# One maximum pass a head instead of one a pair of heads, in a fused attention and feed-forward block

## The chip, the cores and the metric

The kernel runs on one core of a Trainium2 chip. The metric is the device time of one execution in microseconds (us); several executions are timed and their median counts. One further execution is recorded by the hardware profiler. The engines are named as the profile names them: PE is TensorE (PEld its weight loads), DVE is VectorE, ACT is ScalarE, POOL is GpSimd, SP is the queue that issues the DMAs.

## The reference, cut to what matters

For each of 32 batches, `x` has 256 tokens of 128 features. The block normalises `x`, scales and shifts it, and computes an attention in which, for each of 16 heads, the keys and values are read as 8 x 256 matrices, so that the scores of one head are 256 x 256:

```python
q = (x @ Wq + bq).reshape(b, h, dh, t)          # h = 16, dh = 8, t = 256; k and v alike
attn = jnp.einsum('bhdt,bhds->bhts', k, v) * temperature
attn = jax.nn.softmax(attn, axis=-1)
out = jnp.einsum('bhdt,bhts->bhds', q, attn)
```

The result is gated and added to `x`. A second normalisation and a gated feed-forward layer follow, whose activations and weights are rounded block by block to a 4-bit grid, with a second gated residual. The change touches only the row maxima of the scores, which the softmax subtracts.

## The kernel before, in words

The program is a software pipeline over the batches, written out by hand. On each engine a function `step(k, m)` lists in a fixed order the tasks of step k; `at(k, m, lag, task)` runs the task for batch k - lag. So one step works on up to ten batches at once, each at another stage, and each engine executes its list strictly in order. Steps 0 to 11 and those from 32 on are written out; steps 12 to 31 are a hardware loop whose body holds four steps, so the loop turns back at steps 16, 20, 24 and 28. All ordering between engines is by semaphores: a task waits for counts and raises one at its end.

The scores of a head are 256 x 256. PE writes them in `scores` (L900) as two matmuls of 128 x 256 into one of the four slots of `score_ps[:, h % 4]`, a PSUM tensor of four banks, and raises `scored` once a head. A slot may be written again when the exponentials of the head four before are done (`exped`). DVE takes the negated row maxima in `maxes` (L650): pass u reads heads 2u and 2u+1 in one TENSOR_REDUCE of 1024 elements a partition, writes four columns of `neg_max` and raises `maxed`. ACT computes the exponentials in `exps` (L504), two activations of 256 elements a head, each with its row sum, and waits for `maxed` at even heads. PE multiplies them with the scaled queries in `mix` (L942).

The order on DVE in a step is: `var2` (L721), `hid_magic`, maxes 7 of the previous batch, `stats1_rows`, `v_hi`, maxes 0, `h2_max` (L616), `k_lo`, `gate2`, `stats1_end`, `v_lo`, `h2_scale`, maxes 1, `row_sums_inv` (L698), `silu` 0, `h2_recip` (L736), maxes 2, `h2_exponent` (L623), `var1`, `h2_magic`, `silu` 1, maxes 3, `times_up` twice (L757), maxes 4, `hid_max`, maxes 5, `hid_scale`, `gate1` (L704), `hid_recip` (L773), maxes 6, `stats2_rows`, `k_hi`, `stats2_end`, `hid_exponent`.

POOL takes part in a round trip with DVE once a step: `rstd2_pow` (L338) waits for the `ve` of `var2`; `normalise2`, `scale2` and `shift2` (L343, L349, L356) follow; `h2_max` on DVE waits for `shift2`. POOL goes on with `hid_add` and `hid_sub` (L414, L418), `q_scaled` (L369, waits for `row_sums_inv`) and `h2_y` (L389, waits for `h2_recip`); `h2_exponent` on DVE waits for `h2_y`.

On PE the pairs of scores stand between the projections, the transposes and the eight `mix` groups; on ACT the exponentials stand between seven evacuations and activations of other stages. The exponentials of heads 12 to 15 come at the head of the next step. SP issues the DMAs that pass the keys and values through DRAM (`split_dram`) into `k_stack` and `v_stack`, on which the first scores of a batch wait.

Of the kernel before, what the change touches and what calls it, by code (L numbers as in the profile page):

```python
# [10 lines left out]
AX = mybir.AxisListType  # L11

NB, T, D = 32, 256, 128
H, DH = 16, 8
# [19 lines left out]
def adaln_block(nc, x, wq, bq, wk, bk, wv, bv, temperature, w_gate, w_up, w_down, c, wmod, out):  # L34
    with ExitStack() as ctx:
        def sb(name, shape, dt=F32):
            return ctx.enter_context(nc.sbuf_tensor(name, shape, dt))

        def sem(name):
            return ctx.enter_context(nc.semaphore(name))  # L40
# [45 lines left out]
        neg_max = sb("neg_max", [128, 2, H * 2])  # L86
# [19 lines left out]
        score_ps = ctx.enter_context(nc.psum_tensor("score_ps", [128, 4, 2, T], F32))  # L106
# [27 lines left out]
        scored, maxed, exped = sem("scored"), sem("maxed"), sem("exped")  # L134
# [27 lines left out]
        def wait_batches(eng, s, n, per=1):  # L162

            if isinstance(n, int):
                n = min(n, NB)
                if n <= 0:
                    return
            eng.wait_ge(s, n * per)
# [300 lines left out]
        def _(act):  # L469
# [25 lines left out]

            def exps(b, c, h):
                p = c % 2
                if h % 2 == 0:
                    act.wait_ge(maxed, b * (H // 2) + h // 2 + 1)
                if h == 0:  # L500
                    wait_batches(act, mixed, b - 1)
                for a in range(2):
                    n = 2 * h + a
                    nc.scalar.activation(probs[p][:, h, a, :], score_ps[:, h % 4, a, :], ACT.Exp,  # L504
                                         bias=neg_max[:, p, n:n + 1],
                                         accum_out=row_sum[:, p, h, a:a + 1]).then_inc(exped, 1)
# [35 lines left out]
            def step(k, m):  # L542
                at(k, m, 3, exps, 12)
                at(k, m, 3, exps, 13)
                if isinstance(k, int) and k == 5:
                    ff_weights()
                at(k, m, 5, h2T_out)
                at(k, m, 7, hidT_out, 1)
                at(k, m, 3, exps, 14)
                at(k, m, 3, exps, 15)  # L550
                at(k, m, 1, q_out)
                at(k, m, 5, tanh, 0)
                at(k, m, 2, exps, 0)
                at(k, m, 2, exps, 1)
                at(k, m, 2, exps, 2)
                at(k, m, 2, exps, 3)
                at(k, m, 5, tanh, 1)
                at(k, m, 2, exps, 4)
                at(k, m, 2, exps, 5)
                at(k, m, 2, exps, 6)  # L560
                at(k, m, 2, exps, 7)
                at(k, m, 2, exps, 8)
                at(k, m, 2, exps, 9)
                at(k, m, 0, h_out)
                at(k, m, 6, hidT_out, 0)
                at(k, m, 2, exps, 10)
                at(k, m, 2, exps, 11)
# [5 lines left out]
        def _(dve):  # L573
# [69 lines left out]

            def maxes(b, c, u):
                p = c % 2
                dve.wait_ge(scored, b * H + 2 * u + 2)
                if u == 0:
                    wait_batches(dve, exped, b - 1, 2 * H)
                lo = 2 * (u % 2)
                nc.vector.tensor_reduce(neg_max[:, p, 4 * u:4 * u + 4],  # L650
                                        score_ps[:, lo:lo + 2, :, :].rearrange("p b a n -> p (b a) n"),
                                        AX.X, ALU.max, negate=True).then_inc(maxed, 1)

            def stats1_rows(b, c):
                wait_dma(dve, x_loaded, b, c)
# [137 lines left out]
            def step(k, m):  # L793
                if isinstance(k, int) and k == 0:
                    condition()
                at(k, m, 4, var2)
                at(k, m, 6, hid_magic)
                at(k, m, 3, maxes, 7)
                at(k, m, 0, stats1_rows)
                at(k, m, 1, v_hi)  # L800
                at(k, m, 2, maxes, 0)
                at(k, m, 4, h2_max)
                at(k, m, 1, k_lo)
                at(k, m, 7, gate2)
                at(k, m, 0, stats1_end)
                at(k, m, 1, v_lo)
                at(k, m, 4, h2_scale)
                at(k, m, 2, maxes, 1)
                at(k, m, 3, row_sums_inv)
                at(k, m, 5, silu, 0)  # L810
# [252 lines left out]
```

## Time and profile before

| what | us |
|---|---|
| median of 3 runs | 703.82 |
| lowest and highest of them | 703.37, 707.37 |
| the profiled execution | 700.42 |
| its span, first to last instruction | 698.6 |

The profiled execution is 1.8 us longer than its span and 3.4 us shorter than the median. Sums from the trace are made against 700.42 and then carried over to the median.

### The profile page before, as it was taken

To read this page: it belongs to the slowest core of one execution; us is meant where nothing else is said; L and a number is where in the kernel's file an instruction comes from. 1 tells how busy PE (TensorE), PEld (TensorE's weight loads), DVE (VectorE), ACT (ScalarE), POOL (GpSimd) and SP (SyncE) were. 2 spreads that over 40 slices of the span, in tenths; PEclk is the share of its full clock that TensorE was granted. 3 is DMA by queue.
4 is the path that set the end of the run, shared out by engine and by line. 5 is a ranking of instruction groups with operands and counts; after the bars stand their busy time and mean duration, and the time that the engine had idled before them with its cause. 6 is when DMAs were issued, how large, how long until landed. Compare 5 with 4: busy or idle time off the path is not lost.

```text
span 698.6 us, 17168 instructions
## 1 busy us (share of the span) xinstructions
PE 565.0 (81%) x4336; PEld 387.3 (55%) x4336; DVE 600.1 (86%) x1331; ACT 569.5 (82%) x2281; POOL 512.2 (73%) x655
## 2 busy tenths in 40 slices
PE   4577788888888988898888888798888888978673
PEld 2355354656566655665565656565556565645343
DVE  5578489999999999999998999999998999999452
ACT  2287599999998999889997999899997989999211
POOL 2114747888888788878887788878886887877884
PEclk9557799999999999989999999999998999999957
DMA  3544435555555555544554455644555455550000
GB/s 109 148 118 125 122 94 134 144 125 148 139 138 141 146 152 151 133 132 108 149 147 118 126 144 150 153 129 120 132 139 142 116 140 135 144 137 23 31 8 23
DMA packets 87855, 85.82 MB, mean 123 GB/s; under 512 B 8551, under 2 KB 83533, under 8 KB 87789
## 3 DMA queue, kind: packets, MB, share of 16 engines
q1 hardware_dynamic: 87344, 84.94, 46.6%
q14 instruction: 49, 0.39, 0.2%
q8 instruction: 18, 0.29, 0.2%
q10 hardware_dynamic: 444, 0.20, 0.1%
HBM read 47.29 MB, written 37.81 MB: 122 GB/s over the span
## 4 chain that ended last, share of the span: by engine, by line
POOL 26%; issue 24%; DVE 20%; PE 14%; ACT 6%; DMA 5%; SPq 3%; DVEq 1%; ACTq 1%; POOLq 1%
DVE neg_max L650 6%; ACT probs L504 5%; POOL hid_q L414 5%; PE score_ps L900 4%; POOL hid_q L418 4%; PE bank L942 4%; DVE hid L757 3%; POOL rstd L338 3%; DMA k_stack<-split_dram 3%; POOL q_z L369 2%; POOL h_c L349 2%; POOL h L356 2%; DVE hid_am L616 2%; POOL h_c L343 2%; POOL h_q L389 2%
## 5 line engine op out<-in xcount | busy, mean ns | idle before, releaser
L504 ACT ACTIVATE probs<-score_ps,neg_max 128x256 f32<-128x256 f32 x1024 | 471.7, 488 | 43.0 <-DVE neg_max L650 31.8
L650 DVE TENSOR_REDUCE neg_max<-score_ps 128x4 f32<-128x1024 f32 x256 | 310.3, 1213 | 21.6 <-PE score_ps L900 21.1
L900 PE MATMUL score_ps<-v_stack,k_stack 128*128 128x256 f32 x1024 | 220.8, 334 | 61.7 <-DMA k_stack<-split_dram 35.1
L900 PEld LDWEIGHTS score_ps<-v_stack,k_stack 128*128 128x128 f32 x1024 | 155.6, 201 | 134.7 <-ACT probs L504 96.8
L504 ACT ACTIVATION_READ_ACCUMULATOR probs<-score_ps,neg_max 128x1 f32 x1024 | 226.0, 221 | 0.0
L942 PE MATMUL bank<-probs,q_z 128*32 128x256 f32 x2048 | 140.8, 395 | 10.4 <-POOL q_z L369 10.3
L942 PEld LDWEIGHTS bank<-probs,q_z 128*32 128x32 f32 x2048 | 54.6, 111 | 64.8 <-POOL q_z L369 27.8
L962 PE MATMUL bank<-wgu_T,h_T 128*128 128x352 f32 x128 | 56.6, 529 | 24.7 <-DVE ffn_g L788 13.4
L991 PE MATMUL bank<-wd_T,hid_T 118*128 118x128 f32 x384 | 60.6, 299 | 4.8 <-ACT hid_T L538 4.3
L327 POOL TENSOR_TENSOR rstd<-ve,minus_half 128x2 f32<-128x2 f32 x32 | 22.7, 710 | 48.6 <-DVE ve L666 48.5
L991 PEld LDWEIGHTS bank<-wd_T,hid_T 118*128 118x128 f32 x384 | 52.5, 207 | 10.1 <-ACT hid_T L538 8.9
L338 POOL TENSOR_TENSOR rstd<-ve,minus_half 128x2 f32<-128x2 f32 x32 | 29.5, 921 | 37.5 <-DVE ve L721 37.5
L418 POOL TENSOR_TENSOR hid_q<-hid_q,hid_mag 128x704 f32<-128x704 f32 x32 | 53.9, 1683 | 2.5
L414 POOL TENSOR_TENSOR hid_q<-hid_q,hid_mag 128x704 f32<-128x704 f32 x32 | 53.7, 1677 | 2.4 <-DVE hid_mag L627 2.4
L538 ACT ACTIVATE hid_T<-bank 118x384 f32<-118x384 f32 x64 | 32.9, 516 | 23.2 <-PE bank L982 23.1
L971 PE MATMUL bank<-wgu_T,h_T 128*128 128x352 f32 x128 | 50.6, 483 | 0.8 <-DVE kv_lo L691 0.8
L369 POOL TENSOR_TENSOR q_z<-q_T,inv_sum 128x128 f32<-128x128 f32 x64 | 25.0, 411 | 32.6 <-DVE inv_sum L698 32.6
L396 POOL TENSOR_TENSOR hid_q<-hid,hid_rs 128x704 f32<-128x704 f32 x32 | 44.4, 1387 | 3.3 <-DVE hid_rs L773 2.6
L532 ACT ACTIVATE tanh_g<-bank 128x352 f32<-128x352 f32 x64 | 30.4, 475 | 17.4 <-PE bank L962 16.5
L423 POOL TENSOR_TENSOR hid_q<-hid_q,hid_sc 128x704 f32<-128x704 f32 x32 | 44.4, 1389 | 0.2
L377 POOL TENSOR_TENSOR x<-gated,x_in 128x256 f32<-128x256 f32 x32 | 23.2, 726 | 27.9 <-DVE gated L704 27.9
L920 PE MATMUL bank<-w_kv,hT 128*128 128x256 f32 x128 | 40.3, 409 | 1.3 <-ACT hT L514 1.3
(104 smaller groups left out, 919.8 us busy)
## 6 DMA issues: line engine op xcount, KB each, us to landing
split_dram<-kv_hi SPq DMA_DIRECT2D x128, 128.0 KB, 2.4
split_dram<-kv_lo SPq DMA_DIRECT2D x128, 128.0 KB, 2.7
v_stack<-split_dram SPq DMA_DIRECT2D x32, 512.0 KB, 4.3
k_stack<-split_dram SPq DMA_DIRECT2D x128, 128.0 KB, 4.6
mod_bc<-mod_dram SPq DMA_DIRECT2D x32, 256.0 KB, 3.7
x_in<-in_L_attn_x_dram SPq DMA_DIRECT2D x32, 128.0 KB, 3.4
out_dram<-out_t SPq DMA_DIRECT2D x32, 128.0 KB, 1.9
w_mod<-in_L_wmod_dram SPq DMA_DIRECT2D x1, 384.0 KB, 3.4
```

The source lines that it names most:

```text
L338: nc.gpsimd.tensor_tensor(rstd2[:, :], ve2[:, :], minus_half[:, :], ALU.pow).then_inc(rstd2_made, 1)
L396: nc.gpsimd.tensor_tensor(blocks16(hid_q[:, :], 2 * FF), blocks16(hid[:, :], 2 * FF), spread16(hid_rs[:, :], 2 * FF), ALU.mult).then_inc(h ...
L414: nc.gpsimd.tensor_tensor(hid_q[:, :], hid_q[:, :], hid_mag[:, :], ALU.add).then_inc(hid_t_made, 1)
L418: nc.gpsimd.tensor_tensor(hid_q[:, :], hid_q[:, :], hid_mag[:, :], ALU.subtract)\
L423: nc.gpsimd.tensor_tensor(blocks16(hid_q[:, :], 2 * FF), blocks16(hid_q[:, :], 2 * FF), spread16(hid_sc[:, :], 2 * FF), ALU.mult).then_inc ...
L504: nc.scalar.activation(probs[p][:, h, a, :], score_ps[:, h % 4, a, :], ACT.Exp, bias=neg_max[:, p, n:n + 1], accum_out=row_sum[:, p, h, a: ...
L650: nc.vector.tensor_reduce(neg_max[:, p, 4 * u:4 * u + 4], score_ps[:, lo:lo + 2, :, :].rearrange("p b a n -> p (b a) n"), AX.X, ALU.max, n ...
L900: last = nc.tensor.matmul(score_ps[:, h % 4, a, :], k_stack[p][:, h, 128 * a:128 * a + 128], v_stack[p][:, h // R, :], start=True, stop=True)
L942: last = nc.tensor.matmul(bank_mix[32 * g:32 * g + 32, 0:T], q_z[p][:, a, g, r, :], probs[p][:, R * g + r, a, :], start=(i == 0), stop=(i ...
L962: nc.tensor.matmul(bank_gate[a][:, 0:FF], h2_T[:, 128 * a:128 * a + 128], wgu_T[:, 0, :], start=True, stop=True).then_inc(gate_ps_made[a], 1)
L971: nc.tensor.matmul(bank_up[a][:, 0:FF], h2_T[:, 128 * a:128 * a + 128], wgu_T[:, 1, :], start=True, stop=True).then_inc(up_ps_made[a], 1)
L991: last = nc.tensor.matmul(bank_down[:, a * D:(a + 1) * D], hid_T[:, a, t, :], wd_T[:, t, :], start=(t == 0), stop=(t == HT - 1))
```

## The change

Each pass that took the maxima of two heads becomes two passes of one head: 512 elements a partition, two columns of `neg_max`, with a wait and a raised semaphore of their own. A batch has 16 passes in place of 8. ACT waits for `maxed` at every head in place of every second. The place of the passes in the DVE order stays: both halves of a pair stand where the pair stood. PE, POOL and SP are not changed.

```diff
             def exps(b, c, h):
                 p = c % 2
-                if h % 2 == 0:
-                    act.wait_ge(maxed, b * (H // 2) + h // 2 + 1)
+                act.wait_ge(maxed, b * H + h + 1)
...
             def maxes(b, c, u):
                 p = c % 2
-                dve.wait_ge(scored, b * H + 2 * u + 2)
-                if u == 0:
-                    wait_batches(dve, exped, b - 1, 2 * H)
-                lo = 2 * (u % 2)
-                nc.vector.tensor_reduce(neg_max[:, p, 4 * u:4 * u + 4],
-                                        score_ps[:, lo:lo + 2, :, :].rearrange("p b a n -> p (b a) n"),
-                                        AX.X, ALU.max, negate=True).then_inc(maxed, 1)
+                for h in (2 * u, 2 * u + 1):
+                    dve.wait_ge(scored, b * H + h + 1)
+                    if h == 0:
+                        wait_batches(dve, exped, b - 1, 2 * H)
+                    nc.vector.tensor_reduce(neg_max[:, p, 2 * h:2 * h + 2], score_ps[:, h % 4, :, :],
+                                            AX.X, ALU.max, negate=True).then_inc(maxed, 1)
```

## Rows read from the trace of the kernel before

**Rows 1.** the page's part 1: busy us, share of the span, instructions

```profile
PE 565.0 (81%) x4336; PEld 387.3 (55%) x4336; DVE 600.1 (86%) x1331; ACT 569.5 (82%) x2281; POOL 512.2 (73%) x655
```

**Rows 2.** DVE and ACT groups by shape: busy us, mean ns | idle before, releasers

```profile
L504 ACT ACTIVATE probs<-score_ps,neg_max 128x256 f32<-128x256 f32 x1024 | 471.7, 488 | 43.0 <-DVE neg_max L650 31.8 <-issue 8.3
L650 DVE TENSOR_REDUCE neg_max<-score_ps 128x4 f32<-128x1024 f32 x256 | 310.3, 1213 | 21.6 <-PE score_ps L900 21.1
...
L757 DVE TENSOR_TENSOR hid<-silu_g,bank 128x352 f32<-128x352 f32 x64 | 30.3, 513 | 0.5 <-PE bank L971 0.5
...
L616 DVE TENSOR_REDUCE h_am<-h 128x16 f32<-128x256 f32 x32 | 13.4, 418 | 16.4 <-POOL h L356 16.1
```

**Rows 3.** timeline of VectorE, one regular batch: start us, us, instruction [idle before]

```profile
321.73 0.42 DVE L616 TENSOR_REDUCE h_am<-h 128x16 f32<-128x256 f32 x1 [0.60 <-POOL h L356]
...
325.26 1.16 DVE L650 TENSOR_REDUCE neg_max<-score_ps 128x4 f32<-128x1024 f32 x1
326.45 0.29 DVE L623 TENSOR_SCALAR h_mag<-h_q 128x256 int32<-128x256 int32 x1
...
328.73 0.94 DVE L757 TENSOR_TENSOR hid<-silu_g,bank 128x352 f32<-128x352 f32 x2
329.59 1.22 DVE L650 TENSOR_REDUCE neg_max<-score_ps 128x4 f32<-128x1024 f32 x1
330.72 0.88 DVE L616 TENSOR_REDUCE hid_am<-hid 128x44 f32<-128x704 f32 x1
...
333.07 0.42 DVE L773 RECIPROCAL hid_rs<-hid_sc 128x44 f32<-128x44 f32 x1
333.47 1.22 DVE L650 TENSOR_REDUCE neg_max<-score_ps 128x4 f32<-128x1024 f32 x1
```

**Rows 4.** timeline of GpSimd and TensorE in the same batch

```profile
325.80 0.62 POOL L389 TENSOR_TENSOR h_q<-h,h_rs 128x256 f32<-128x256 f32 x1
...
332.71 0.72 PE L900 MATMUL score_ps<-v_stack,k_stack 128*128 128x256 f32 x4
```

**Rows 5.** the chain that ended last, a regular batch: start us, us, what

```profile
413.44 0.18 DVE ve L721
...
419.37 1.45 POOL hid_q L418
...
421.79 0.59 POOL h_q L389
...
432.19 0.18 DVE ve L721
```

**Rows 6.** timeline of VectorE, the instruction that writes ve at L721

```profile
108.92 0.17 DVE L721 TENSOR_SCALAR ve<-mv 128x2 f32<-128x2 f32 x1
...
373.76 0.17 DVE L721 TENSOR_SCALAR ve<-mv 128x2 f32<-128x2 f32 x1 [0.34 <-issue]
...
394.84 0.17 DVE L721 TENSOR_SCALAR ve<-mv 128x2 f32<-128x2 f32 x1
...
643.70 0.17 DVE L721 TENSOR_SCALAR ve<-mv 128x2 f32<-128x2 f32 x1
```

**Rows 7.** the chain at a turn of the loop

```profile
366.94 1.14 DVE neg_max L650
...
372.85 2.17 issue
...
377.11 0.80 PE score_ps L900 x2
...
391.21 0.18 DVE hid_sc L620
```

**Rows 8.** the chain while the pipeline fills

```profile
80.45 1.15 DVE neg_max L650
```

**Rows 9.** timeline of VectorE in the first step after the loop

```profile
577.68 1.23 DVE L650 TENSOR_REDUCE neg_max<-score_ps 128x4 f32<-128x1024 f32 x1 [0.27 <-PE score_ps L900]
```

**Rows 10.** timeline of VectorE in the turn step

```profile
380.69 0.73 DVE L620 TENSOR_SCALAR h_sc<-h_am 128x16 f32<-128x16 f32 x1
```

## The prediction, made before the changed kernel was timed

> **What bounds the kernel now.** I first read the engines' busy times [rows 1]: DVE leads with 600.1 us of 698.6, ACT and POOL have 569.5 and 512.2. A share alone doesn't say who sets the pace, so the second view is the length of one step, from one `ve` at L721 to the next. Between the rows at 108.92 and 643.70 [rows 6], the first and the last of 29 such rows, there are 28 steps. The 22 regular ones take 18.3 to 19.0 us, 410.5 us together. The four at which the loop turns take 21.1 to 21.6 (373.76 to 394.84 is one of them), and the steps that enter and leave the loop 19.7 each.
>
> Third comes the chain of waits through a regular step [rows 5]. It leaves DVE at `ve` (413.44), runs through POOL (second normalisation, `hid_sub` until 420.8, `h_q` at 421.79), comes back to DVE and stays there, with no stall of note, until the next `ve` at 432.19. So a regular step is one trip: some 8.9 us from `ve` to the end of `h_q`, all POOL's, then 9.8 us of DVE work. While POOL has the trip, DVE does its other work and has a little over: it sits idle 0.60 us before `h_am` [rows 3], and all such waits are 16.1 us [rows 2]. The second slack is negative: the pass of maxes 2 starts at 325.26 and `h_mag` at 326.45, 1.19 later, where the pass of maxes 4 lets its successor start after 1.13 (329.59 to 330.72) [rows 3]. The 0.06 is `h_mag` waiting for `h_q`, whose end is at 326.42 [rows 4]. ACT has 17.8 us of work in a step of 18.7 and isn't on the chain there.
>
> At a turn it is otherwise [rows 7]: the pass of maxes 4 (366.94) releases ACT, ACT works through until it stands still for 2.17 us of issue (372.85), then come its next exponentials, the scores of the new batch on PE (377.11) and PE's mixes, and DVE enters only at `hid_sc` (391.21).
>
> **The change: the price of a split pass on DVE.** A TENSOR_REDUCE takes 1213 ns for 1024 elements and 418 ns for 256 [rows 2], so 1.035 ns an element and about 0.15 us fixed; one of 512 should take 0.68 us. What a step pays is the distance between starts, not the duration. The pass at 329.59 lasts 1.22, and the next instruction starts after 1.13, 0.09 before its end. The two passes of `times_up` show the same for two equal instructions that read PSUM, each with its wait: 513 ns one [rows 2], 0.94 both [rows 3], so the second starts 0.43 after the first, again 0.08 before its end. I therefore put a half pass at 0.68 - 0.09 = 0.59 to 0.60, a pair at 1.19 in place of 1.13: **0.06 us more a pair**, 0.5 us for the eight of a batch, though the added busy time will read as 8 x 0.15 = 1.2 us a batch, some 35 to 40 us in all. The bounds: nothing, if starts could follow at the bare 0.53; and 0.15, if the second half waited for the end of the first (0.68 + 0.60 - 1.13).
>
> That upper bound has a page behind it. The rows show overlap of 0.08 to 0.09 us between neighbours [rows 3]. The Trainium skill, "VectorE: DVE Perf Modes", section "The DRAIN you can't avoid", says that the next operation doesn't start until the pipe has emptied, and its errata section that many small tiles pay the fixed cost once each; by its figure of (N+151)/0.96 ns a half pass would be 0.69 us and a pair dearer by 0.157. By that rule this is the slow rival below; the rows of `times_up` speak against it.
>
> The four pairs in DVE's own part of the trip (maxes 3 to 6) cost 4 x 0.06 = 0.25 (with 0.063 unrounded). Maxes 7 and 0 stand before `h_am` and fall into the 0.60 of idle time; if that were gone they would cost 0.13. Maxes 1 and 2 stand between `h_am` and `h_mag`, where 0.06 is free: 0.13 - 0.06 = 0.07. Against this, maxes 6 start at 333.47, 0.40 after `hid_rs`, which lasts 0.42 and would let go after 0.33; its scores end on PE at 333.43 [rows 3, 4]. The first half needs only the first head, done 0.36 us before, so some 0.05 comes back. **A regular step gets 0.25 + 0.07 - 0.05 = 0.27 us longer.**
>
> **What starts earlier.** The first half of a pair is ready at 0.60 where the pair was ready at 1.13: ACT may begin 0.53 us earlier wherever the chain passes from DVE to ACT. Each turn has one such handover, maxes 4 at 366.94 [rows 7]. After it DVE is off the chain until 391.21. So the regular step before a turn and the turn together change by 0.07 + 0.06 (maxes 1 to 3) - 0.53 + 0.06 (maxes 6) = -0.34. While the pipeline fills, the chain has three such places of which I show one, the pass at 80.45, behind which ACT comes [rows 8]: 3 x 0.53, less a few added 0.06, is -1.3. In the step after the loop maxes 2 stood waiting for the scores of the second head (577.68, 0.27 us [rows 9]); with the first half done meanwhile about 0.3 is saved.
>
> **ACT's added waits** (8 a batch, ahead of the odd heads). Behind one stand the exponentials of that head and all later ones, and PE's scores four heads on wait for them. The second half is done 0.60 after the first, while the two exponentials of the even head (488 ns each [rows 2], started one after the other) keep ACT for 0.9 to 1.0, so the wait is met when it is reached: nothing in the middle, up to a few 0.01 us each as a bound, 1 us in all where ACT is on the chain. If DVE had other work between the halves that cover would be gone; it has none. The orders on PE, POOL and SP and all DMAs are as before. The semaphore arithmetic of the second half runs on DVE's sequencer while the first half is in the engine, as it does for the second `times_up`.
>
> **Sum.** Of the 22 regular steps four go with a turn and one ends in the loads of keys that set the entry into the loop; 17 remain: 17 x 0.27 = +4.6. Four turns: -1.4. After the loop -0.3. Fill -1.3. The tail after 643.70 goes through POOL and PE and has hardly a maximum in it: 0. Together +1.6 us: 702.0 in a profiled execution of the kind that had 700.42, and 705.4 against the median of 703.82.
>
> **The rivals.** *The fixed cost is paid in full* (0.15 us a pair): DVE's own part +0.60, maxes 1 and 2 +0.24, less 0.05, is 0.8 a step; the pairs before `h_am` still hide (0.30 of 0.60). 17 x 0.8 = +13.4, the turns and the fill together about -1.5: 716. For it: the duration has the fixed part, and DVE is the busiest engine. Against it: the overlap seen between neighbours. It would also come about if the added wait held the second half back by some 0.09 us; this decides from about 0.1 us a pair (17 x 0.5 - 3 = +5.5, near the line of slower by 1%). Chance 0.2.
>
> *The earlier start is worth more than I count.* ACT waited 31.8 us for maxima and DVE 21.1 us for scores [rows 2]. If half of DVE's waits and the handovers shortened the chain, and ACT's earlier exponentials moved PE ahead in regular steps too, 27 waits x 0.4 = 10.8 us come off and +6 go on (22 x 0.27): -5, 699; with ACT's share up to -9, 695. Against it: in regular steps POOL's trip sets the time from `ve` to `h_mag`, and no earlier ACT shortens that. Chance 0.13.
>
> *A late DVE meets POOL.* In the turn step `h_sc`, 16 elements a partition, took 0.73 us [rows 10], until POOL's running operation ended; if the shifts of 0.1 us put a DVE operation behind a POOL operation in regular steps, this costs about 1 us in each, +15. No regular step stands that near, since `h_am` restarts DVE at POOL's beat. Chance 0.05.
>
> **How the numbers follow.** My forecast, within a few us of +1.6, has 0.62. A difference under 1%, 7 us, can hardly be told from no change here. Within the forecast nearly all lies within 1%; the fast rival puts 0.08 beyond 1% and the rest inside; the slow ones lie mostly beyond: faster 0.08, same 0.71, slower 0.21. The range leaves out the far half of the slow rivals and the far end of the fast one: 699 to 714.
>
> **What would show it.** In the profile after: 512 passes of about 0.68 us; two halves of a pair starting 0.60 apart; regular steps of 18.9 to 19.0 us in place of 18.6 to 18.7; idle time before `h_am` down from 0.60 to about 0.47; ACT's wait for maxima well under 31.8 us; turns 0.3 shorter or equal. Starts 0.68 apart would show the slow rival. I'm wrong if the chain of a regular step no longer goes by POOL's trip, or if ACT's added waits show as gaps between exponentials.

## The result: 2.3% slower, and the profile after

The changed kernel took 721.32 us (median of 4, 720.68 to 721.95) against 704.7 for the kernel before; the ratio is 1.0231, with a 95% interval of 1.0197 to 1.0265. The profiled execution took 720.68 with a span of 718.9 us, 20.3 more than before. I had forecast +1.6 us, and the time lies outside my range. Every ratio below is against the kernel before as it was timed beside that run, whose median lay between 700.38 and 704.7 us, and it leaves out executions in a slower state of the chip (there was one, 710.35 us of unrolled_before, which its median includes).

The page's line of busy times, and its line for the queue that brings instructions (packets, MB, share of 16 DMA engines):

```profile
PE 568.7 (79%) x4336; PEld 386.3 (54%) x4336; DVE 609.5 (85%) x1587; ACT 569.6 (79%) x2281; POOL 514.0 (71%) x655
...
q14 instruction: 74, 0.61, 0.3%
```

The same queue on the page of the kernel before:

```profile
q14 instruction: 49, 0.39, 0.2%
```

DVE's busy time grew by only 9.4 us [rows 1], since time in which two neighbours overlap counts once in it. What stands out is the queue of instructions, with 74 packets in place of 49. The groups that answer to [rows 2]:

```profile
L503 ACT ACTIVATE probs<-score_ps,neg_max 128x256 f32<-128x256 f32 x1024 | 473.1, 495 | 55.3 <-DVE neg_max L649 43.5 <-issue 8.2
L649 DVE TENSOR_REDUCE neg_max<-score_ps 128x2 f32<-128x512 f32 x512 | 325.2, 677 | 8.4 <-PE score_ps L898 8.3
...
L755 DVE TENSOR_TENSOR hid<-silu_g,bank 128x352 f32<-128x352 f32 x64 | 30.3, 514 | 0.2
...
L615 DVE TENSOR_REDUCE h_am<-h 128x16 f32<-128x256 f32 x32 | 13.4, 419 | 17.2 <-POOL h L356 17.0
```

A half pass takes 677 ns (I had 0.68). The idle time before DVE's passes fell from 21.6 to 8.4 us, but ACT waits more for maxima, 43.5 us in place of 31.8. A regular batch on DVE, to be held against [rows 3] and [rows 6]:

```profile
321.50 0.17 DVE L719 TENSOR_SCALAR ve<-mv 128x2 f32<-128x2 f32 x1
...
325.76 0.42 DVE L615 TENSOR_REDUCE h_am<-h 128x16 f32<-128x256 f32 x1 [0.49 <-POOL h L356]
...
329.35 1.22 DVE L649 TENSOR_REDUCE neg_max<-score_ps 128x2 f32<-128x512 f32 x2
330.48 0.29 DVE L622 TENSOR_SCALAR h_mag<-h_q 128x256 int32<-128x256 int32 x1
...
331.62 1.29 DVE L649 TENSOR_REDUCE neg_max<-score_ps 128x2 f32<-128x512 f32 x2
332.82 0.95 DVE L755 TENSOR_TENSOR hid<-silu_g,bank 128x352 f32<-128x352 f32 x2
333.68 1.29 DVE L649 TENSOR_REDUCE neg_max<-score_ps 128x2 f32<-128x512 f32 x2
334.88 0.88 DVE L615 TENSOR_REDUCE hid_am<-hid 128x44 f32<-128x704 f32 x1
...
340.25 0.17 DVE L719 TENSOR_SCALAR ve<-mv 128x2 f32<-128x2 f32 x1
```

Two half passes keep DVE for 1.20 us where the pass took 1.13 (331.62 to 332.82, 333.68 to 334.88), and for 1.13 ahead of `h_mag` (329.35 to 330.48). The idle time before `h_am` is 0.49 in place of 0.60. The step, from 321.50 to 340.25, takes 18.75 us; the same step before, from 317.49 to 336.09, took 18.60. So regular steps changed by even less than forecast. The time is lost where the loop turns:

```profile
377.68 0.50 DVE L622 TENSOR_SCALAR hid_mag<-hid_q 128x704 int32<-128x704 int32 x1
384.04 0.17 DVE L719 TENSOR_SCALAR ve<-mv 128x2 f32<-128x2 f32 x1 [5.86 <-issue]
```

`ve` is the first operation of the loop's body on DVE. It starts 5.86 us late, and for nothing that another engine does: the wait is put down to issue, time in which the profile shows nothing that the engine waited for. In [rows 6] the same instruction at the same turn (373.76) waited 0.34. The chain of waits at this turn has the records of DVE's sequencer too (DVEq); L191 is the line of the loop, and the first of its records is the jump back:

```profile
377.76 0.06 DVEq L191
377.82 3.67 issue
381.50 0.07 DVEq L191
...
381.75 2.18 issue
...
384.04 0.18 DVE ve L719
```

So DVE stands still twice: for 3.67 us right behind the jump, then it works off three instructions (one of L191, two waits on semaphores), and stands still again for 2.18. The other three turns show the same, 3.50 to 4.01 and 2.09 to 2.35 us. The waits by issue in the loop, 240 to 560 us, which holds the four turns (us in total, times, longest), after:

```profile
DVE ve L719 <- issue: 23.8, 4, 6.4
...
ACT probs L503 <- issue: 8.2, 4, 2.5
```

and before:

```profile
ACT probs L504 <- issue: 8.3, 4, 2.3
...
DVE ve L721 <- issue: 1.4, 4, 0.4
```

Instructions that arrived during one trip through the loop, `ve` to `ve`, after (403.6 to 485.9) and before (317.5 to 394.8):

```profile
q14 instruction: 11, 0.09, 0.4%
```

```profile
q14 instruction: 5, 0.04, 0.2%
```

A packet has 8 KB. Before the change a trip brought 5 packets, afterwards 11. The loss is in the four pairs of steps around a turn: from the last `ve` ahead of each turn to the second behind it the kernel before took 40.0, 40.0, 40.1 and 40.5 us, the changed one 45.2, 44.5, 44.6 and 46.3. That is 20.1 us more, out of 20.3. The rest cancels: the fill is 3.4 us shorter (the `ve` at which [rows 6] start stands at 105.51 in place of 108.92), and all other steps and the tail together are 3.6 us longer.

### The profile page after: what moved, and what is told of

Its sections match the earlier page's. It is cut to its first block, busy times and chain, and to the rows that moved or that the text cites. A ratio compares the mean times of both kernels' runs of the same rounds, so it can differ in the third digit from the quotient of the medians.

```text
span 718.9 us, 17744 instructions
## 1 busy us (share of the span) xinstructions
PE 568.7 (79%) x4336; PEld 386.3 (54%) x4336; DVE 609.5 (85%) x1587; ACT 569.6 (79%) x2281; POOL 514.0 (71%) x655
## 4 chain that ended last, share of the span: by engine, by line
DVE 30%; issue 24%; POOL 15%; PE 13%; DMA 7%; ACT 5%; SPq 4%; DVEq 1%; ACTq 1%; POOLq 1%
DVE neg_max L649 15%; ACT probs L503 4%; PE bank L940 3%; DMA k_stack<-split_dram 3%; PE score_ps L898 3%; POOL rstd L338 3%; POOL h_c L349 2%; POOL h L356 2%; DVE hid L755 2%; DMA split_dram<-kv_lo 2%; SPq L252 2%; POOL h_c L343 2%; PE bank L960 2%; DVE stats L710 2%; DVE hid_am L615 1%
## 5 line engine op out<-in xcount | busy, mean ns | idle before, releaser
L503 ACT ACTIVATE probs<-score_ps,neg_max 128x256 f32<-128x256 f32 x1024 | 473.1, 495 | 55.3 <-DVE neg_max L649 43.5
L649 DVE TENSOR_REDUCE neg_max<-score_ps 128x2 f32<-128x512 f32 x512 | 325.2, 677 | 8.4 <-PE score_ps L898 8.3
L898 PE MATMUL score_ps<-v_stack,k_stack 128*128 128x256 f32 x1024 | 215.5, 330 | 63.5 <-ACT probs L503 31.4
L503 ACT ACTIVATION_READ_ACCUMULATOR probs<-score_ps,neg_max 128x1 f32 x1024 | 233.1, 228 | 0.0
L898 PEld LDWEIGHTS score_ps<-v_stack,k_stack 128*128 128x128 f32 x1024 | 152.6, 200 | 137.8 <-ACT probs L503 99.9
L960 PE MATMUL bank<-wgu_T,h_T 128*128 128x352 f32 x128 | 57.9, 539 | 35.1 <-DVE ffn_g L786 20.5
L969 PE MATMUL bank<-wgu_T,h_T 128*128 128x352 f32 x128 | 54.3, 513 | 1.3 <-DVE kv_lo L689 1.3
L960 PEld LDWEIGHTS bank<-wgu_T,h_T 128*128 128x128 f32 x128 | 22.3, 214 | 42.4 <-issue 41.2
L423 POOL TENSOR_TENSOR hid_q<-hid_q,hid_sc 128x704 f32<-128x704 f32 x32 | 44.5, 1390 | 0.2
L980 PE MATMUL bank<-ident,hid_q 128*118 128x128 f32 x192 | 33.3, 287 | 11.6 <-POOL hid_q L423 8.5
```

Of the source, the lines that this page charges most:

```text
L423: nc.gpsimd.tensor_tensor(blocks16(hid_q[:, :], 2 * FF), blocks16(hid_q[:, :], 2 * FF), spread16(hid_sc[:, :], 2 * FF), ALU.mult).then_inc ...
L649: nc.vector.tensor_reduce(neg_max[:, p, 2 * h:2 * h + 2], score_ps[:, h % 4, :, :], AX.X, ALU.max, negate=True).then_inc(maxed, 1)
L898: last = nc.tensor.matmul(score_ps[:, h % 4, a, :], k_stack[p][:, h, 128 * a:128 * a + 128], v_stack[p][:, h // R, :], start=True, stop=True)
L960: nc.tensor.matmul(bank_gate[a][:, 0:FF], h2_T[:, 128 * a:128 * a + 128], wgu_T[:, 0, :], start=True, stop=True).then_inc(gate_ps_made[a], 1)
L969: nc.tensor.matmul(bank_up[a][:, 0:FF], h2_T[:, 128 * a:128 * a + 128], wgu_T[:, 1, :], start=True, stop=True).then_inc(up_ps_made[a], 1)
```

## The experiments

All twelve kernels compute the whole result. The tool is an unused instruction, an increment of a semaphore that nobody reads, put where an engine is idle, so that all later instructions of that engine stand further back in its program:

```diff
+            for _ in range(55):
+                dve.sem_inc(pad_dve, 1)
             def condition():
...
             def step(k, m):
+                if isinstance(k, int) and k == 2:
+                    for _ in range(55):
+                        dve.sem_inc(pad_dve, 1)
```

Counted in the program, DVE's loop body, which one trip through the loop works off, has 329 instructions before the change and 393 after it: 32 passes more and, since every wait in the loop compares with a value that must be worked out from the loop's counter, 32 register instructions more. It stands behind 620 instructions before and behind 699 after, by the 79 passes that the written-out steps ahead of it have more. ACT's body grows from 365 to 397, its reads of the row sums counted as instructions of their own.

**Is it the place or the length?** First, the shift of the changed kernel.

> The changed kernel with 110 increments of an otherwise unused semaphore on DVE, 55 at its start and 55 ahead of step 2, where DVE is idle; nothing else differs. They move the loop body in DVE's instruction stream from starting behind 699 instructions to behind 809 and do not change its 393 instructions. Theory A (where the body lies): the 5.6 to 6.4 us that DVE stands still at each turn of the loop are a reload of the body's first instructions, needed because the body touches three blocks of 256 instructions; behind 809 instructions it touches two. The stall falls to about 0.3 us, the turns to about 21 us, and the time to 702 to 707. Theory B (size): a body of 393 instructions is too long by itself; the stall stays near 6 us and the time at 719 to 724. Theory C (something else at the turn, as ACT's additional waits): time as changed, 719 to 724, with the stall of DVE still shown.

Measured: 701.31 us, ratio 1.0021 (1.0002 to 1.0040). Nearly all of the loss is gone, with every split pass and every added wait in place. The waits by issue in its loop:

```profile
DVE ve L723 <- issue: 12.2, 4, 3.3
...
ACT probs L504 <- issue: 9.5, 4, 2.5
```

DVE's went from 23.8 to 12.2 us, about 3 a turn and not 0.3, so theory A was right in that the place matters, and wrong in its size of the remaining stall. Theories B and C, by which nothing would change, are out. Its partner was to produce the stall in the kernel before.

> The kernel before, maxima in pairs, with 85 such increments on DVE (43 and 42): its loop body of 329 instructions starts behind 705 in place of 620 and so ends behind 1034, in a third block of 256. Theory A: the stall of about 6 us appears at each of the four turns, the turns and their next steps take 4 to 6 us more, 720 to 726 in all. Theory B: the body is as short as before, no stall, 703 to 706. Theory C: as B.

Measured: 698.87 us, ratio 0.9972 (0.9947 to 0.9996), DVE's wait unchanged:

```profile
DVE ve L725 <- issue: 1.5, 4, 0.4
```

I had expected 720 to 726. Theory A in this form, with blocks of 256 counted from the start of the program, fell.

> The kernel before with 60 such increments on ACT, 30 at the head of each of its steps 0 and 1. By my count ACT's loop body (365 instructions, its row sums counted as instructions of their own) starts behind some 757 and touches three blocks of 256; with 60 more it touches two. Theory A: ACT's 1.6 to 2.2 us of issue at each turn go, the turns take 19 to 20 us in place of 21, and the time falls to 693 to 700. Theory B: ACT's stall is the price of any turn and stays, 703 to 706.

Measured: 702.6 us, ratio 1.0031 (1.0008 to 1.0055), ACT's stalls of some 2 us all there. A miss: by the same blocks I had expected 693 to 700.

> The changed kernel with both: 110 increments on DVE and 60 on ACT. Theory A: neither engine stalls at the turn by more than 0.5 us, and the time is that of the first run less what ACT's shift is worth, 694 to 702. Theory B: 719 to 724, both stalls in place.

Measured: 702.39 us, ratio 1.0035 (1.0014 to 1.0055): as the first run, with nothing from ACT's shift, and just above the 694 to 702 expected. DVE's waits by issue are 11.9 us and ACT's 9.0.

**A finer rule.** The instruction packets have 8 KB. Before the change 5 come in a trip, some 26 us apart where ACT runs without a stall, in which time ACT works off about a third of its 365 instructions, so a packet would hold 128. The Trainium skill, "Perfetto Trace Analysis", section "The 4-stage abstract model", gives an instruction 64 bytes. By that, 8 KB are 128 instructions, which agrees with the trace. The new theory: an engine keeps three such packets and one fetched ahead. A body within three packets is never fetched again; one that reaches into a fourth has its first packet replaced, and the jump back must wait for it.

> The kernel before with 72 increments on DVE (36 and 36) where the run with 85 showed nothing. The traces show instructions coming in packets of 8 KB, 128 instructions of 64 bytes, and in one turn of the loop 5 such packets before the change and 11 after. Theory A2: an engine can jump back without a reload only if its loop body lies within three such packets; counted so, DVE's body of 329 starts 43 to 55 instructions into a packet in the kernel before and 0 to 12 into one with 85 more, both within three; with 72 more it starts at 115 to 127 and touches four. So DVE stalls 2.5 to 6.5 us at each turn, packets go to 10 or 11 a turn, and the time rises by 2 to 18 us over before. Theory B2 (only the size counts, more than some 361 to 384 instructions): no stall, 5 packets, time as before within 3 us.

Measured: 704.99 us, ratio 1.0001 (0.9976 to 1.0025). In the trace:

```profile
DVE ve L725 <- issue: 12.6, 4, 3.3
...
ACT probs L505 <- issue: 9.0, 4, 2.4
```

```profile
q14 instruction: 10, 0.08, 0.4%
```

Packets and stall came as theory A2 had it, from a shift of 72 where 85 had given nothing. Here DVE waits once at a turn, right behind the jump:

```profile
375.62 2.96 issue
378.57 0.07 DVEq L192
...
379.04 0.18 DVE ve L725
```

The time did not move: DVE's 3 us stand beside ACT's own stall of 2.2 us at the same turn, which held the chain in the kernel before [rows 7]. Now the chain goes by ACT's stall at the first turn and by DVE's at the other three, and the pairs of steps around a turn still take 40.2 to 40.6 us, against 40.0 to 40.5. The lower end of my expectation, +2 us, was too high.

> The kernel before with 80 increments on ACT (40 and 40). The times of the packets place ACT's body of 365 instructions 52 to 64 into a packet, so it touches four, and with 60 more it still did, which is why that run kept the stall. With 80 more it starts at 4 to 16 and, by theory A2, fits in three: ACT's 1.6 to 2.7 us of issue at the turns vanish, packets fall from 5 a turn to 0 to 2, the turns take 19 us in place of 21, time 4 to 9 us under before. Theory B2: 365 instructions are too many wherever they lie, nothing changes.

Measured: 694.89 us, ratio 0.9881 (0.9832 to 0.9931). In the loop ACT no longer waits for issue at all; all its waits in the view over the same 240 to 560 us are

```profile
ACT probs L505 <- DVE neg_max L654: 12.8, 32, 0.9
ACT q_T L521 <- PE bank L937: 3.1, 4, 1.2
ACT tanh_g L533 <- PE bank L966: 1.1, 2, 0.7
```

and from 320 to 390 us the only queues that moved anything are the queue of data and a second queue of instructions, with 16 KB in its packet:

```profile
q1 hardware_dynamic: 9570, 9.41, 51.1%
q8 instruction: 1, 0.02, 0.1%
```

Not one packet of q14, the queue counted so far, came in 70 us: DVE's and ACT's loops both stay in place. Eighty idle instructions make the kernel before 1.2% faster, where sixty made it no faster.

**The sharp tests.** By the rule, DVE's body starts 43 to 48 instructions into a packet before the change and 122 to 127 into one after it. This is worked out from the runs with 79 and 85: 6 instructions further on, the body has to start in the next packet. At most 6 instructions are left in a packet at 122 to 127, so a second packet is needed at once behind the first.

> The changed kernel with only 10 unused increments on DVE (5 and 5). The stalls so far: DVE starting its body, by my placement, 122 to 127 instructions into a packet of 128 (the changed kernel) stalls about 6 us, 104 to 120 in about 3 us, 43 to 55 or 0 to 5 in, with a body of 329, not at all. Ten more move the changed kernel's start to 4 to 9 instructions into the next packet; its 393 still touch four packets. Theory A2 (place): the 6 us stall falls to about 3 us, which ACT's own stall covers, and 10 increments give back 15 us or more: 700 to 706. Theory B2 (the stall comes with the length of the body and the 110 increments helped some other way, as by their time in the fill): 716 to 724.

Measured: 707.34 us, ratio 1.0069 (1.0039 to 1.0098). Ten idle instructions give back 1.6 of the 2.3%. The four waits are 3.1 to 3.8 us:

```profile
DVE ve L723 <- issue: 13.9, 4, 3.8
```

It came out just above the expected 706, and by the ratios 3 to 4 us above the run with 110.

> The kernel before, pairs, with 79 increments on DVE (40 and 39): its body then starts exactly where the changed kernel's does, behind 699 instructions. 72 increments gave a 3 us stall and no loss of time, 85 no stall. Theory A2: the stall is about 6 us, as in the changed kernel, 10 or 11 packets a turn, and the time 714 to 722, the whole loss without one split pass. Theory B2: 701 to 706, at most the 3 us stall.

Measured: 714.33 us, ratio 1.0174 (1.0130 to 1.0218). The timeline of DVE at the turn:

```profile
378.07 0.50 DVE L627 TENSOR_SCALAR hid_mag<-hid_q 128x704 int32<-128x704 int32 x1
383.92 0.17 DVE L725 TENSOR_SCALAR ve<-mv 128x2 f32<-128x2 f32 x1 [5.35 <-issue]
```

and the chain there:

```profile
378.21 3.05 issue
381.26 0.07 DVEq L192
...
381.52 2.29 issue
...
383.92 0.18 DVE ve L725
```

The stall is 5.35 us, again in two parts with the same three instructions between them, as at the other three turns (2.98 to 3.01 and 2.09 to 2.11 us). So three quarters of the change's loss appears in a kernel that has no split pass and no added wait. It lies at the same place: the four pairs of steps around a turn are 13.7 us longer than in the kernel before.

> The changed kernel with one wait for both heads ahead of the two passes, each of which still raises the semaphore, so that ACT may start after the first; DVE's body is 361 instructions, and 12 increments (6 and 6) put its start 6 to 11 into a packet, so it fits in three. Theory A2: no DVE stall over 0.5 us, about 5 packets a turn, all ACT's, and with ACT's stall of 2.2 us still there 700 to 706. Theory B2: as the changed kernel in stall, 3 to 6 us, if the border lies under 361 instructions.

```diff
-                for h in (2 * u, 2 * u + 1):
-                    dve.wait_ge(scored, b * H + h + 1)
-                    if h == 0:
-                        wait_batches(dve, exped, b - 1, 2 * H)
+                dve.wait_ge(scored, b * H + 2 * u + 2)
+                if u == 0:
+                    wait_batches(dve, exped, b - 1, 2 * H)
+                for h in (2 * u, 2 * u + 1):
```

Measured: 701.94 us, ratio 0.9998 (0.9975 to 1.0022). The wait of `ve` is back at 1.5 us, and a trip brings 5 packets:

```profile
DVE ve L723 <- issue: 1.5, 4, 0.4
```

```profile
q14 instruction: 5, 0.04, 0.2%
```

**What the passes themselves cost.** Two runs have no loop at all, and one has a loop in which neither engine fetches again.

```diff
-            with eng.Fori(LOOP_FROM, LOOP_TO - UNROLL + 1, UNROLL) as k:
-                for u in range(UNROLL):
-                    step(k + u, (LOOP_FROM + u) % 4)
+            for k in range(LOOP_FROM, LOOP_TO):
+                step(k, k % 4)
```

> The kernel before with steps 12 to 31 written out, no loop on any engine. Both theories: no turns, no stall at ACT or DVE; the four turns and the entry and exit go from 19.7 to 21.6 us to about 18.6, 10 to 12 us less: 688 to 694. If the running fetch of a long program costs, as PE's, the gain is smaller, and issue waits show in every step.

Measured: 698.61 us, ratio 0.9881 (0.9827 to 0.9934). By the ratio some 8 us, a little less than the 10 to 12 expected: the turns are gone, but single steps of 20 to 21 us remain between those of 18.44. Some of what holds them up are the loads of `x`, for which DVE waits here 9.9 us between 240 and 560 us, and 1.9 us in the kernel before:

```profile
DVE stats L656 <- DMA x_in<-in_L_attn_x_dram: 9.9, 10, 2.1
```

> The changed kernel with steps 12 to 31 written out. It shows what the split passes cost and give without any loop. By the terms of my prediction a regular step is 0.2 to 0.3 us longer than in the same kernel in pairs and the fill up to 1.5 to 3 us shorter: 3 to 7 us over the unrolled kernel before, ratio 1.004 to 1.010 between the two. A theory by which the passes themselves cost the 17 us expects 1.02 or more.

Measured: 696.59 us, ratio 0.9892 (0.9841 to 0.9943). Against unrolled_before that is 1.001, under the 1.004 to 1.010 expected; but with intervals of half a per cent on either no difference of this size can be told. The regular steps are 18.60 us in place of 18.44. A theory by which the passes themselves cost the 17 us is out: it expected 1.02 or more.

> The price of the passes by themselves, with neither engine reloading: two passes a pair behind one wait, ACT waiting once a pair for the second, 12 increments on DVE, 80 on ACT. The pair of half passes costs 0.06 us more and gives nothing back. Its partner is the kernel before with 80 increments on ACT (ratio to before 0.988). By the terms of my prediction a regular step is 0.3 us longer and the step where ACT waits for maxima 0.06: 5 to 8 us over its partner, ratio to before 0.995 to 1.000, no stall in the trace. If the fixed cost were paid in full (0.15 us a pair) the ratio would be 1.008 or more.

Its edit on ACT, against the changed kernel; on DVE it is that of one_wait_split:

```diff
-                act.wait_ge(maxed, b * H + h + 1)
+                if h % 2 == 0:
+                    act.wait_ge(maxed, b * H + h + 2)
```

Measured: 697.17 us, ratio 0.9929 (0.9902 to 0.9955). Its partner is act_80 with 0.9881, so the passes cost some 0.5%, 3 us, a little under the 5 to 8 expected, and no more than the two intervals together. The traces have it more sharply: one trip through the loop takes 75.5 us in place of 75.0.

| kernel | split | DVE's body: behind, length | ACT shift | DVE's issue waits in the loop, us | ratio |
|---|---|---|---|---|---|
| before | no | 620, 329 | 0 | 1.4 | 1 |
| before_72 | no | 692, 329 | 0 | 12.6 | 1.0001 |
| before_79 | no | 699, 329 | 0 | 20.7 | 1.0174 |
| shifted_before | no | 705, 329 | 0 | 1.5 | 0.9972 |
| act_shifted_before | no | 620, 329 | 60 | 1.4 | 1.0031 |
| act_80 | no | 620, 329 | 80 | 1.4 | 0.9881 |
| the change | yes | 699, 393 | 0 | 23.8 | 1.0231 |
| split_10 | yes | 709, 393 | 0 | 13.9 | 1.0069 |
| shifted_split | yes | 809, 393 | 0 | 12.2 | 1.0021 |
| both_shifted_split | yes | 809, 393 | 60 | 11.9 | 1.0035 |
| one_wait_split | yes | 711, 361 | 0 | 1.5 | 0.9998 |
| split_cost_only | yes | 711, 361 | 80 | 1.5 | 0.9929 |

## Why the prediction was wrong, step by step

**What bounds the kernel.** Right for regular steps: POOL's trip and DVE's own work still set them. From `ve` to the end of `h_q` it is 8.94 us after (321.50 to 330.44) and 8.93 before. The idle time before `h_am` fell as forecast (0.49 where I had 0.47), and a pair that keeps DVE for 1.20 us has nearly the predicted size, 1.19. The rival in which the fixed cost is paid in full is refuted. That its +12 us lies nearer to the result is a coincidence of numbers. The 0.157 us a pair that the prediction worked out for it from a figure of the Trainium skill ("VectorE: DVE Perf Modes", the errata section) was not measured either: the figure stands there for an addition of two tensors, and the maxima here cost 0 to 0.07 us a pair.

**A regular step +0.27 us.** The sign was right, the size too large: 0.10 to 0.15 in the loop, 0.16 written out. Not all pairs cost 0.06; the pairs of maxes 2 and of maxes 6 cost nothing, as 329.35 to 330.48 shows for the former. In the step shown, the part up to `h_mag`, for which I had +0.07, grew by 0.02, and DVE's own part, for which I had +0.20, by 0.13. The busy time that I expected to grow by 35 to 40 us grew by 9.4, since the profile's page counts overlapping neighbours once.

**What starts earlier.** The fill gave back more than my 1.3 us: 3.4 in this pair of traces, some 2 over all of them. The `ve` at 108.92 stands at 108.1 to 108.6 in the other kernels with pairs and at 106.1 to 106.6 in the other kernels in which ACT may start after the first half; where it has to wait for both (split_cost_only) it stands at 108.45, so the gain is ACT's earlier start. ACT's wait for maxima, which I expected well under 31.8 us, is 43.5, but only with the stall: in shifted_split it is 21.5, in before_79 54.2.

With the loss at the turn removed by place alone, the change is worth +0.2% (shifted_split), my +1.6 us; one_wait_split and the two written-out kernels say the same within their intervals. That it fits so well is partly luck: the regular steps cost less than I had, the fill gave more, and the turns gave less (four of them -0.5 us in one_wait_split, +1.6 with the stall that is left in shifted_split, where I had -1.4).

**The step that failed** is "Four turns: -1.4". I took a turn to be a fixed price of ACT's, 2.17 us of issue, from which the earlier start would come off, and weighed the added instructions only by the time in which they run. Wrong was the silence about where instructions come from: the sum has no term for it. The added 64 instructions lengthened DVE's body from 329 to 393 and, through those in the written-out steps ahead of it, moved its start by 79. The first made a body that is kept in some places into one that was fetched again at each trip in all three places tried; the second put its start, by the rule above, at the end of a packet, and DVE waits twice. Shown are: that place alone produces 1.7% in the kernel before (before_79), that place alone removes 1.6 to 2.1% from the changed one (split_10, shifted_split), and that a shorter body in a fitting place has no stall (one_wait_split). The four turns, with the steps ahead of them, cost +20.1 us where I had -1.4. My term for "the semaphore arithmetic" was right as to its running time, zero, and blind to its length: half of the added instructions are such.

It could have been asked of the profile before. ACT's 2.17 us of issue at the turn against DVE's 0.34 [rows 6 and 7] was a sign that one engine's loop was fetched again and the other's not, and the instruction queue's packets in one trip, 5, showed that something was fetched in each. The Trainium skill, "Runtime: NRT & Kernel Launch", section "Instruction fetch mechanics", states that a taken branch whose target isn't in the pages held waits for a DMA of the target page. The runs agree: each of DVE's stalls begins right behind the jump. The same section of the Trainium skill has pages of 256 instructions, two of them held. That does not fit the runs, wherever the first page starts. The kernels in pairs stall with 72 and 79 and not with 85, so by that rule a page would have to begin with a body that stands behind 705 instructions, or at most five instructions ahead of it; then split_10's 393 instructions would lie within two pages and not stall, and they stall for 3.1 to 3.8 us. The traces show 8 KB packets, and a limit that fits three packets of 128. The measurement decides.

**What stays open.** That the 6 us are two waits one behind the other is shown by the records between them, at all eight turns of the changed kernel and of before_79. That each of them ends with the arrival of a packet is argued: from the place of the body's start, and from the four packets of q14 that came in the changed kernel between 459.9 and 466.3 us, which don't say whose they are. The rule of three packets and one fetched ahead tells right, for DVE and ACT, in all twelve kernels with a loop whether they stall, though the place of each engine's program in its packets was itself worked out from runs; that nothing else could tell as well is not shown. Why the first of the two waits is longer in the changed kernel (3.50 to 4.01 us) than in before_79 (2.98 to 3.05) is open, and with it a part of the difference between 2.31% and 1.74%; another part is the passes' own cost. What the change would be worth with ACT's loop also kept in place was not tried: with a wait at every head ACT's body has 397 instructions, by the rule too many for three packets in any place.

## What to carry to other kernels

Count an edit inside a hardware loop in instructions too, with the register arithmetic of every wait, on each engine that it touches, and look at the issue waits of the first instruction of the body and at the instruction queue's packets before and after. A loop body near a limit can go from free to 5 or 6 us a turn by a few instructions anywhere ahead of it (79 and 85 idle ones here), so a change measured as slower may be a harmless one in a bad place: shift it by some idle instructions before judging it. The same look at the kernel before the change found 1.2% that had nothing to do with the maxima (act_80, 694.89 us, the fastest kernel here by ratio, together with the one written out), and a stall on one engine may be covered by another's at the same turn, as in before_72, so each must be seen alone.

## What the runs showed of the hardware that I had not expected

Instructions come in packets of 8 KB. A body of 329 instructions on DVE, and one of 365 on ACT, is kept from trip to trip in some places and fetched again in others, 72 and 79 against 85 idle instructions ahead of it, 60 against 80. Where it is fetched again, the engine stands still at the turn: about 2.2 us on ACT (2.17 at one turn), 2.8 to 3.8 on DVE, and 5.1 to 6.4 on DVE, in two parts with three instructions between them, where by the rule above the body starts within the last few instructions of a packet. What the engine shows is not all of the fetch: in the trace before, ACT's sequencer takes the jump back at 370.69 us and its next instruction at 375.02, 4.3 us later, but ACT has work at hand until 372.85, so only 2.17 show. In act_80 there are 0.2 us between the two records at each turn. Two half passes of 512 elements that follow each other cost between nothing and 0.07 us more than one of 1024, though each has a duration of 0.68 against 1.21.
